# Half chunks first, a padded last chunk and products by pairs in a three-layer interaction network

## The reference

```python
x0 = inputs; prev = inputs; results = []
for i, f in enumerate([128, 128, 128]):
    h = prev.shape[1]
    Wr = Ws[i].reshape(h, M, f)
    z = relu(einsum('bhk,bmk,hmf->bfk', prev, x0, Wr) + bs[i][None, :, None])
    half = f // 2
    results.append(z[:, :half])      # the first 64 channels are kept
    prev = z[:, half:]               # the last 64 feed the next layer
pooled = sum(concatenate(results, axis=1), axis=-1)
return pooled @ W_lin
```

## Time and profile before

| | us |
|---|---|
| median of 3 runs | 2056.39 (2055.49 to 2056.47) |
| profiled execution, own time | 2055.68 |
| its span | 2053.9 |
| TensorE busy | 2030.3 (99%) |
| VectorE busy | 1809.6 (88%) |
| ScalarE busy | 539.0 (26%) |
| granted TensorE clock, mean | 0.997 |

### The profile page before, as it was taken

The page is one execution under the profiler, slowest core; times in us unless marked ns, Lnnn a source line. Parts: engine busy times, 40 slices in busy tenths (PEclk is TensorE's granted clock), DMA queues, the critical chain, the costliest instruction groups (busy, mean ns, idle before and its releaser), DMA issues.

```text
span 2053.9 us, 20773 instructions
## 1 busy us (share of the span) xinstructions
PE 2030.3 (99%) x6050; PEld 804.6 (39%) x6050; DVE 1809.6 (88%) x1630; ACT 539.0 (26%) x547; POOL 1.2 (0%) x5
## 2 busy tenths in 40 slices
PE   7999999999999999999999999999999999999998
PEld 2344333443333443334433344333344333443342
DVE  6988988889988889888899888898888988889987
ACT  1331133311333212333113332123321233311322
POOL 0000000000000000000000000000000000000000
PEclk9999999999999999999999999999999999999999
DMA  8967866668766688666786666876668866668710
GB/s 199 199 146 163 179 145 140 148 146 190 158 130 150 144 176 169 150 139 144 157 190 142 140 147 143 187 166 133 147 145 168 183 141 141 145 148 190 152 38 0
DMA packets 98550, 308.99 MB, mean 150 GB/s; under 512 B 19252, under 2 KB 19252, under 8 KB 98408
## 3 DMA queue, kind: packets, MB, share of 16 engines
q1 hardware_dynamic: 97400, 307.71, 68.7%
q10 hardware_dynamic: 1136, 1.12, 0.2%
HBM read 308.74 MB, written 0.01 MB: 150 GB/s over the span
## 4 chain that ended last, share of the span: by engine, by line
PE 89%; DVE 6%; issue 3%; ACT 0%; DVEq 0%
PE acc L323 66%; PE acc L362 20%; DVE prod L210 4%; PE acc L317 3%; DVE prod L212 2%; ACT prev L404 0%; DVE sum L258 0%; DVE x_bc L189 0%; DVEq L241 0%; PE acc_y L393 0%; DVE x_rot L201 0%; ACT res L434 0%; DVE x_seed L305 0%; ACT pool L439 0%; DVEq L240 0%
## 5 line engine op out<-in xcount | busy, mean ns | idle before, releaser
L210 DVE TENSOR_TENSOR prod<-prev,x_bc 128x1024 f32<-128x1024 f32 x1216 | 1390.1, 1223 | 221.6 <-ACT prev L404 215.0
L323 PE MATMUL acc<-prod,w_sb 128*128 128x512 f32 x2432 | 1052.3, 593 | 0.3 <-DVE prod L210 0.3
L323 PEld LDWEIGHTS acc<-prod,w_sb 128*128 128x128 f32 x2432 | 459.4, 190 | 592.6 <-issue 546.8
L362 PE MATMUL acc<-prod,w_sb 128*64 128x512 f32 (+1 forms) x2560 | 569.3, 596 | 6.1 <-DVE prod L212 1.2
L323 PE MATMUL acc<-x_rot,w_sb 117*128 117x512 f32 (+1 forms) x768 | 341.0, 599 | 2.7 <-DVE x_rot L201 2.7
L362 PEld LDWEIGHTS acc<-prod,w_sb 128*64 128x64 f32 (+1 forms) x2560 | 175.3, 136 | 396.2 <-issue 320.1
L409 ACT ACTIVATE prev<-acc,bias 32x1024 f32<-32x1024 f32 x256 | 283.4, 1107 | 4.0
L404 ACT ACTIVATE prev<-acc,bias 64x1024 f32<-64x1024 f32 x128 | 142.0, 1109 | 498.6 <-PE acc L317 355.2
L201 DVE TENSOR_TENSOR x_rot<-x_rot,x_rep 117x1024 f32<-117x1024 f32 (+1 forms) x192 | 221.1, 1220 | 3.0 <-DMA x_rot<-x 2.9
L323 PEld LDWEIGHTS acc<-x_rot,w_sb 117*128 117x128 f32 (+1 forms) x768 | 143.4, 190 | 198.8 <-issue 189.7
L439 ACT ACTIVATE pool<-sum,wl_col 128x64 f32 (+1 forms) x65 | 22.1, 342 | 679.6 <-DVE sum L258 679.6
(11 more groups left out here) (17 smaller groups left out, 21.8 us busy)
## 6 DMA issues: line engine op xcount, KB each, us to landing
x_bc<-x SPq DMA_DIRECT2D x310, 256.0 KB, 13.1
x_bc<-x SPq DMA_DIRECT2D x155, 512.0 KB, 21.2
x_rot<-x SPq DMA_DIRECT2D x192, 312.0 KB
x_rot<-x SPq DMA_DIRECT2D x192, 156.0 KB
x_bc<-x SPq DMA_DIRECT2D x124, 128.0 KB, 8.9
x_rep<-x SPq DMA_DIRECT2D x64, 192.0 KB
x_rep_s<-x SPq DMA_DIRECT2D x64, 128.0 KB, 2.6
x_rot_s<-x SPq DMA_DIRECT2D x64, 128.0 KB, 2.8
```

The costliest lines, as they stand in the source:

```text
L210: mul = nc.vector.tensor_tensor(prod[:, slot, :], old[:], new, ALU.mult)
L323: mm = nc.tensor.matmul(acc[:, h, :], w, rhs[:, BANK * h:BANK * h + BANK], start=start, stop=stop)
L362: mm = nc.tensor.matmul(acc2[HALF * h:HALF * h + HALF, :], w2_sb[0:k, c, :], prod[0:k, c % RING, BANK * h:BANK * h + BANK], start=(c == 0) ...
```

## The change

1. **Order of chunks** (`ORDER`). In layers 1 and 2 the 64-pair chunk is now position 0, and the other 19 follow.
2. **Layer 0's split chunk moves.** The split chunk of block i + 1 is multiplied right behind layer 1's own split chunk of block i (`layer0_split`, called from `layer1`), and no longer ahead of layer 0's full chunks. Its product (`product_split`) is made ahead of layer 1's products, and its loads (`load_split`) have a semaphore of their own.
3. **Layer 2's 64-pair chunk is padded.** The lower half of its weights is zeroed once by GpSimd, its product is made in all 128 rows, and its matmul is 128 rows high like the others.
4. **Products by pairs** (`RUNS`). Eight pairs of chunks in each of layers 1 and 2 are one VectorE instruction of 2048 elements, with the `prev` operand repeated; four chunks remain single (in layer 1 the first of them is two half instructions). Waits on `prod_ready` now count these 12 runs. TensorE waits for a chunk's run; VectorE waits for as many free slots as the run has chunks.
5. **Ends.** Blocks 0 and 1 are written out ahead of the loop. In the first block the seeds of the tiles are shuffled in another order. In the last two blocks the cut is after 12 chunks of layer 2 (8 runs).

```diff
+    ORDER = [CH - 1] + list(range(CH - 1))
+    RUNS = [(0, 1), (1, 1), (2, 2), (4, 2), (6, 2), (8, 2), (10, 1), (11, 1), (12, 2), (14, 2), (16, 2), (18, 2)]
+    RUN_OF = [n for n, (_, w) in enumerate(RUNS) for _ in range(w)]
+    NR = len(RUNS)
...
-    TAIL = RING + 1
+    TAIL_RUNS, TAIL = 8, 12
...
+            sp.wait_ge(split_used, 2)
+            load_split(2)
+            sp.wait_ge(acc0_full, 2)
+            load_pairs(2)
+            sp.wait_ge(prod_ready, 2 * NR)
+            load_bc(2, 0)
...
+            def product_split(i):
 
                 dve.wait_ge(split_loaded, i * (32 * NH) + 32 * NH)
                 nc.vector.tensor_tensor(x_rot_s[:], x_rot_s[:], x_rep_s[:], ALU.mult).then_inc(prod0_ready, 1)
...
+            def product(layer, n, u, phase=0):
+
+                pos, w = RUNS[n]
+                a, t = CHUNKS[ORDER[pos]]
+                s = (phase + pos) % RING
                 old, new = prev[layer - 1][a], x_bc[:, u, t, :]
...
+                if w == 2:
+                    twice = old[:].rearrange("p (o n) -> p o n", o=1).to_broadcast([P, w, NB])
+                    mul = nc.vector.tensor_tensor(prod[:, s:s + w, :], twice, x_bc[:, u, t:t + w, :], ALU.mult)
+                elif layer == 1 and t == T1:
+                    for h in range(NH):
+                        k, cols = slice(HALF * h, HALF * h + HALF), slice(BANK * h, BANK * h + BANK)
+                        mul = nc.vector.tensor_tensor(prod[k, s, cols], old[k, cols], new[k, cols], ALU.mult)
                 else:
...
+                    mul = nc.vector.tensor_tensor(prod[:, s, :], old[:], new, ALU.mult)
                 mul.then_inc(prod_ready, 1)
 
             def products1_seeded():
 
...
+                spread = {0: 1, 1: 2, 2: 4, 3: 6, 4: 8, 5: 10, 6: 12}
+                late = {2: (6,), 3: (7, 8), 4: (T2,)}
+                for n, (pos, w) in enumerate(RUNS):
+                    if n in spread:
+                        dve.wait_ge(seed_spread, spread[n])
+                    if pos in (0, 11):
+                        dve.wait_ge(prev_ready[0], 1 if pos == 0 else 2)
+                    dve.wait_ge(chunk_used, pos + w)
+                    product(1, n, 0)
+                    for t in late.get(n, ()):
+                        seed(t)
...
+                    product_split(i + 1)
                     products1(i, u, j + u, i * (2 * CH))
                     channel_sum2(i)
                     products0(i + 1)
                     products2(i, u, i * (2 * CH) + CH)
...
+            pool.wait_ge(w2_loaded, 16)
+            nc.gpsimd.memset(w2_sb[HALF:P, CH - 1, :], 0.0).then_inc(w2_ready, 1)
...
+            def layer1(i, runs, phase=0, ahead=True):
                 pe.wait_ge(res01_ready, i * 2 + 1)
...
+                for pos, c in enumerate(ORDER):
+                    pe.wait_ge(prod_ready, runs + RUN_OF[pos] + 1)
+                    s = (phase + pos) % RING
+                    if pos == 0:
+                        split(acc1, w1_sb[:, c, :], [prod[0:HALF, s, 0:BANK], prod[HALF:P, s, BANK:NB]],
+                              True, False).then_inc(chunk_used, 1)
+                        if ahead:
+                            pe.wait_ge(res01_ready, i * 2 + 2)
+                            layer0_split(i + 1)
                     else:
...
+                        full(acc1, w1_sb[:, c, :], prod[:, s, :], False, pos == CH - 1).then_inc(chunk_used, 1)
+
+            def layer2(i, runs, part=range(CH)):
                 pe.wait_ge(res2_ready, i + 1)
...
+                for pos in part:
+                    pe.wait_ge(prod_ready, runs + RUN_OF[pos] + 1)
                     for h in range(NH):
...
+                        mm = nc.tensor.matmul(acc2[HALF * h:HALF * h + HALF, :], w2_sb[:, ORDER[pos], :],
+                                              prod[:, pos % RING, BANK * h:BANK * h + BANK],
+                                              start=(pos == 0), stop=(pos == CH - 1))
```

More of the change, by code:

```diff
@@ L101, in cin_kernel @@
         rot_loaded = [sem(f"rot_loaded{g}") for g in range(len(X0_GROUPS))]
-        bc_loaded = [[sem(f"bc_loaded{u}{g}") for g in range(len(XB_GROUPS) + 1)]
+        bc_loaded = [[sem(f"bc_loaded{u}{g}") for g in range(len(XB_GROUPS) + 2)]
                      for u in range(U)]
@@ L164, in _ @@
             load_bc(1, 1)
[L165 to L169, removed]
+            sp.wait_ge(split_used, 2)
[4 more added lines that the diff above has]
+            load_bc(2, 0)
+            sp.wait_ge(split_used, 3)
+            load_split(3)
+            sp.wait_ge(acc0_full, 3)
+            load_pairs(3)
+            sp.wait_ge(prod_ready, 4 * NR)
+            load_bc(3, 1)
             with sp.Fori(1, STEPS - 1) as j:
@@ L201, in products0 @@
                         nc.vector.tensor_tensor(r, r, x_rep[0:ROWS0[c], :], ALU.mult).then_inc(prod0_ready, 1)
[L202 to L207, removed]
-                old, new = prev[layer - 1][a], x_bc[:, u, t, :]
[L209 to L212, removed]
-                else:
-                    for h in range(NH):
-                        k, n = slice(HALF * h, HALF * h + HALF), slice(BANK * h, BANK * h + BANK)
-                        mul = nc.vector.tensor_tensor(prod[k, slot, n], old[k, n], new[k, n], ALU.mult)
+                        if c < len(seeds):
+                            seed(seeds[c])
@@ L234, in products1 @@
                 group = {t0: g for g, (t0, _) in enumerate(XB_GROUPS)}
-                group[T2] = len(XB_GROUPS)
-                for c, (a, t) in enumerate(CHUNKS):
+                group[T1], group[T2] = BC_T1, BC_T2
+                for n, (pos, w) in enumerate(RUNS):
+                    a, t = CHUNKS[ORDER[pos]]
                     if a == 0 and t in group:
                         dve.wait_ge(bc_loaded[u][group[t]], loads * (16 * BC_LOADS[group[t]]))
[L239 to L252, removed]
+                    if pos in (0, 11):
+                        dve.wait_ge(prev_ready[0], i * 2 + (1 if pos == 0 else 2))
+                    dve.wait_ge(chunk_used, first + pos + w)
@@ L253, in products2 @@
+                    product(1, n, u, phase)
+            def products2(i, u, first, part=range(NR)):
+                for n in part:
+                    pos, w = RUNS[n]
+                    if pos in (0, 11):
+                        dve.wait_ge(prev_ready[1], i * 2 + (1 if pos == 0 else 2))
+                    dve.wait_ge(chunk_used, first + pos + w)
+                    product(2, n, u)
+                    if n == TAIL_RUNS:
                         dve.wait_ge(res01_ready, i * 2 + 3)
```

120 lines of the change are left out of this document (59 added, 61 removed).

## The result

| | before | after |
|---|---|---|
| median of 5 runs, us | 2056.39 (2054.95 to 2056.91) | 2065.95 (2064.87 to 2067.17) |
| profiled execution, own time | 2055.68 | 2067.17 |
| its span | 2053.9 | 2065.4 |

The ratio is 1.0048, 95% interval 1.0035 to 1.0061: slower by half a per cent. 2066 was forecast, with 0.74 on slower.

What follows compares the result with a forecast made beforehand. A block was taken as bound by a loop through TensorE, ScalarE and VectorE. First block 3.35 + next step 0.6 + blocks 7.2 - end 1.0 = +10.1 us on 2056.39 gives 2066.5, called 2066; range 2051 to 2078.

Steps and rivals of the forecast that it cites:

- VectorE's part of the loop: Layer 2's products: a pair takes 2.21 us against 2.27, saving 0.52 us over 8 pairs, from 24.69 to 24.17.
- the loop: Layer 1 on TensorE, 2.35 us of ScalarE, 24.7 us of VectorE, two layer 2 chunks on TensorE, layer 1 again.
- TensorE's part: Layer 2's last two chunks through layer 1: +0.72 us with layer 0's half chunk, plus 0.05 waiting at layer 1's head.
- Per block: Each block: +0.72 - 0.52 + 0.05 = +0.25, so 63.29 us; +7.2 us for 29 blocks.
- The first block: Layer 1 of the first block: TensorE waits for pairs made between seed shuffles, 0.4, 1.1 and 1.4; +3.35 us.
- The step to the next block: From the first block's last layer 1 pass to the next block's: bound by TensorE, +0.6 us.
- The end: Last block and half chunks around it: pairs -0.5, padding -0.14, ScalarE's earlier start and chunk order -0.2 each; -1.0 us.
- The start: Before the first block's layer 1 products, up to 37.03 us: set by loads and unchanged.
- Of the rivals, the first: Layer 2: VectorE's part shrinks until TensorE's path decides; faster from pairs of about 2.165, about 2048 at 2.13; chance 0.12.
- the other side: TensorE's path with the wait at layer 2's last chunks quite gone: 62.4 us a block, about 2041.
- The second: VectorE products: pairs save nothing because the first operand is read twice; +0.5 us per block, 2081; chance 0.08.
- The third rival: Same mechanism, cheaper: pair 2.20, half chunk in time, first block's waits taken up; 2060, partly 2058 to 2062; chance 0.18.

Runs made afterwards that it cites:

- experiment 1: The changed kernel with its pairs taken back, every chunk's product a VectorE instruction of its own again; 2079.42 us, 1.0117 of the kernel before.
- 8: The kernel before with only the 8 pairs in layer 2's products, without the padding; 2044.31 us, ratio 0.9946.
- experiment 2: The changed kernel with layer 0's half chunk back at the head of layer 0; 2050.22 us, 0.9977 of the kernel before.
- experiment 6: The kernel before with only layer 2's last chunk padded to 128 rows; 2051.69 us, ratio 0.9982.
- experiment 10: The changed kernel, with block 1's half-chunk loads late, and the first block's seeds spaced out; 2061.32 us, 1.0029 of the kernel before.
- the second comparison: The changed kernel run once more, unaltered, against the kernel before on the same chip; 2063.79 us, ratio 1.0045.
- experiment 7: The kernel before with the padded chunk and 8 pairs in layer 2's products only; 2040.14 us, ratio 0.9927.
- experiment 11: The changed order with VectorE making half of layer 1's first spread, and the first block's seeds spaced; 2041.12 us, 0.9927 of the kernel before.

## Why the prediction was right

Term by term, forecast against the profiles:

- **VectorE's part of the loop.** A pair was put at 2.21 and takes 2.20. From the last pass of layer 1 to layer 2's last two chunks it is 1053.82 - 1026.69 = 27.13 us (27.16 forecast, 27.68 before). Experiments 1 and 8 isolate it.
- **TensorE's part.** From there to the next last pass it is 63.24 - 27.13 = 36.11 (36.13 forecast, 35.37 before). Experiment 2 shows the half chunk to be what adds, experiment 6 that a saved switch subtracts.
- **Per block** that is +0.196 where +0.25 was forecast, 5.7 us over 29 blocks for 7.2. The difference is in no one step: -0.55 for -0.52, and +0.74 for +0.77 at the other end, each within the rounding of the rows.
- **The first block** costs 41.06 - 37.59 = 3.47 (3.35 forecast), and experiment 10 shows 2.62 of it to be the places of the seeds. Of the 0.84 that stay, 0.38 is the wait for the first pair. With single products and the seeds close together (experiment 1) the block still costs 2.68 more than before, so the pairs are the smaller part. The step to the next block is +0.65 for +0.6.
- **The end** is 1.0 shorter (from block 30's spread to the span's end, 89.3 against 90.3), for -1.0.
- **The start** was said to stay. In the first profile it came 2.66 us later, in the next one 0.69 earlier: it varies from run to run, and that profile was also the longest of the five runs. What the early loads add is open.

Without the start the terms measured sum to 3.47 + 0.65 + 5.7 - 1.0 = 8.8, where 10.1 was forecast, and the two comparisons give 9.6 and 8.3. So the mechanism and the terms hold, but that the median fell on 2066 to the tenth is partly luck. The blocks were put 1.5 us too high, 2066.5 was rounded down to 2066, and the first comparison lies 0.8 above the terms. By the second comparison 2066 is 1.3 us too high.

Of the rivals, the first (it needed a pair of 2.165 or less) is refuted by the 2.20 in the rows; what it said of the other side was right, as the kernel without the channel sum went to 62.353 a block where 62.4 was given. The second needed pairs 2.27 apart, and experiment 1 shows the saving in full: 0.069 us a pair, so no cost of the repeated operand is seen. The third rival had three conditions. A pair of 2.20 came true, but the half products were not quite in time at the head (1.91 us after the last pair, where 1.87 would do), and the first block's waits were not taken up (3.47 us more there), so its 2058 to 2062 did not come.

One thing the forecast did not ask. Parts 3 and 4 of the change, with pairs in layer 2 alone, bring 0.50 us a block on the old order (experiment 7). Parts 1 and 2 take back 0.69: part 2 alone 0.49 (experiment 2), and the other 0.20 is one more switch. Experiment 7, the old order with padding and pairs, is 0.9927 of the kernel before. No version that computes the whole output was faster; experiment 11 reaches the same ratio with the new order.

## What to carry to other kernels

Find the loop before judging an edit: follow one period from engine to engine by starts, and ask of each piece of work whether it lies on the loop or beside it. An engine that is 98% busy need not be the bound, and moving its work from beside a wait to where all wait for it costs the whole piece, here 0.95 us to save one switch that was hidden. When a fix brings two paths level, test the parts alone: two of them may be worth more than all.

## What was not expected of the hardware

The landing of the first loads differs between profiles by up to 4.7 us (layer 0 of the first block ended between 32.7 and 37.4 us in thirteen profiles, whose first loads are not all alike; 37.37 and 34.02 in the two of the changed kernel itself), while the mean block in the middle repeats to 0.005 us across chips and runs of kernels with the same loop (63.242, 63.240, 63.242, 63.237). Effects under 2 us are therefore better read from a stretch of the profile than from medians.
